# Score masks written by ScalarE into the scores' PSUM slot, in place of eight bfloat16 mask products a tile

## What is computed

```
mask = (it < jb) | (it > jb + w) | (jb == -1)
sim = jnp.einsum('bhwie,bhwje->bhwij', bq, bk2) * QK_SCALE
sim = jnp.where(mask, -jnp.finfo(sim.dtype).max, sim)
attn = jax.nn.softmax(sim, -1)
...
for i in range(DEPTH):
    x = attn_layer(shift_tokens(x), Wqkv[i], q_scale[i], k_scale[i], Wo[i]) + x
    x = ffn_layer(shift_tokens(x), ln_g[i], ln_b[i], W1[i], b1[i], W2[i], b2[i]) + x
```

## Time and profile before

| | |
|---|---|
| median of 3 runs | 3268.82 us (3267.74 to 3269.96) |
| the profiled execution's own time | 3261.97 us |
| its span | 3260.2 us |
| mean granted TensorE clock | 0.99 |
| busy share: TensorE, its weight loads, VectorE, ScalarE, GpSimd | 95%, 73%, 84%, 72%, 75% |
| instructions | 117935 |

### The profile page before, as it was taken

One profiled execution on the slowest core, in us unless ns is written; L12 is line 12 of the kernel. 1 busy time (PEld: TensorE's weight loads), 2 busy tenths in 40 slices (PEclk: granted clock), 3 DMA queues, 4 the chain that ended last, 5 costly groups with the idle time before them and its releaser, 6 DMA issues.

```text
span 3260.2 us, 117935 instructions
## 1 busy us (share of the span) xinstructions
PE 3101.1 (95%) x50166; PEld 2366.0 (73%) x50166; DVE 2741.3 (84%) x2887; ACT 2360.4 (72%) x3182; POOL 2442.6 (75%) x1239
## 2 busy tenths in 40 slices
PE   6999999999999999998888899999999999999998
PEld 5777787787777777775333677777777777777776
DVE  6888788888888888886999888788888888888886
ACT  5777777777777777666776677677777777777665
POOL 5778678687777777672899877777778778778764
PEclk8999999999999999999999999999999999999999
DMA  3333243243243243231000333333433433423322
GB/s 111 90 104 82 71 107 89 67 108 86 70 107 85 70 107 72 63 73 30 35 1 9 92 79 73 95 77 75 101 74 78 101 73 77 103 69 81 72 68 66
DMA packets 160006, 252.08 MB, mean 77 GB/s; under 512 B 50749, under 2 KB 52990, under 8 KB 157182
## 3 DMA queue, kind: packets, MB, share of 16 engines
q1 hardware_dynamic: 159486, 244.54, 30.0%
HBM read 35.67 MB, written 7.34 MB: 13 GB/s over the span
## 4 chain that ended last, share of the span: by engine, by line
PE 78%; POOL 6%; DVE 6%; issue 5%; ACT 4%; DMA 0%; SPq 0%; DVEq 0%; ACTq 0%; POOLq 0%
PE PS L327 14%; PE PS L428 10%; PE PS L230 10%; PE PS L232 9%; PE PS L231 9%; PE PS L379 8%; PE PS L543 3%; PE PS L502 2%; PE PS L503 2%; PE PS L504 2%; PE PS L389 2%; POOL ARENA L1908 2%; PE PS L487 2%; DVE ARENA L1715 2%; PE PS L459 1%
## 5 line engine op out<-in xcount | busy, mean ns | idle before, releaser
L1799 POOL TENSOR_TENSOR ARENA<-ARENA,RN 128x1024 f32<-128x1024 f32 x192 | 364.7, 1899 | 477.7 <-ACT RN L957 470.5
L230 PE MATMUL PS<-WL,XH 128*128 128x512 f32 x1536 | 673.5, 438 | 28.7 <-DVE ARENA L1404 24.1
L327 PE MATMUL PS<-C,ARENA 128*128 128x128 f32 x4608 | 621.0, 278 | 34.6 <-POOL ARENA L1799 11.2
L327 PEld LDWEIGHTS PS<-C,ARENA 128*128 128x128 f32 x4608 | 520.4, 142 | 161.5 <-issue 99.2
L232 PE MATMUL PS<-WH,XH 128*128 128x512 f32 x1536 | 608.9, 396 | 0.0
L231 PE MATMUL PS<-WH,XL 128*128 128x512 f32 x1536 | 604.4, 393 | 0.0
L1791 POOL TENSOR_TENSOR ARENA<-ARENA 128x1024 f32<-128x1024 f32 x192 | 469.2, 2444 | 167.8 <-DVE ARENA L1363 167.2
L1785 POOL TENSOR_TENSOR ARENA<-ARENA 128x1024 f32<-128x1024 f32 x192 | 460.0, 2396 | 13.0 <-DVE ARENA L1345 13.0
L1813 POOL TENSOR_TENSOR ARENA<-ARENA,RI 128x1024 f32<-128x1024 f32 x192 | 366.2, 1907 | 41.4 <-DVE RI L1415 31.3
L428 PE MATMUL PS<-ARENA 128*32 128x128 f32 x12288 | 378.6, 274 | 5.9 <-issue 1.7
L1807 POOL TENSOR_TENSOR ARENA<-ARENA,RN 128x1024 f32<-128x1024 f32 x192 | 372.6, 1940 | 10.4 <-ACT RN L957 10.4
(11 more groups left out here) (170 smaller groups left out, 6148.5 us busy)
## 6 DMA issues: line engine op xcount, KB each, us to landing
ARENA<-ARENA SPq DMA_DIRECT2D x1536, 64.0 KB
ARENA<-VT SPq DMA_DIRECT2D x1536, 64.0 KB
ARENA<-in_wqk SPq DMA_DIRECT2D x24, 512.0 KB, 5.9
ARENA<-in_wvo SPq DMA_DIRECT2D x6, 1024.0 KB, 6.1
MD<-ARENA SPq DMA_DIRECT2D x6, 1024.0 KB, 8.0
ARENA<-MD SPq DMA_DIRECT2D x6, 1024.0 KB, 9.7
ARENA<-in_w SPq DMA_DIRECT2D x12, 341.0 KB
ARENA<-in_w SPq DMA_DIRECT2D x12, 192.0 KB, 2.8
```

Source lines behind the costliest of these rows:

```text
L230: nc.tensor.matmul(o, XH[:, x], WL[:, s], start=True, stop=False)
L327: last = nc.tensor.transpose(PS[:, slot, 128 * j:128 * j + 128], src[:, 128 * j:128 * j + 128], ident)
L1799: nc.gpsimd.tensor_tensor(a, a, bc(RN[:, n % 2, 0:16], 64), ALU.mult).then_inc(q_nrm, 1)
```

## The change

`score_masks` and `MK` go, and with them VectorE's cast at the start. The host's constants now hold two masks in float32 of 128 rows by 64 columns, `mask` and `mask0` (the second for the first tile of the sequence). ScalarE copies one of them, broadcast over the 16 heads, into slot 3 (`set_masks`), and the score products add to what stands there. TensorE waits for that copy (`masks_set`) where it waited for what had freed the slot; those waits are ScalarE's now. `set_masks` stands at one of two places in a step of ScalarE: right behind k_evacuate (`early`), or, for tiles of class 3, tile 0 and the merge tiles, behind keep_merged. In the closing part the write of tile 95 (slot 0) stands ahead of the exponential of tile 94.

The additions rely on flags that TensorE keeps: a product with `start=True` marks its whole bank as not yet written. That is why the merge products and the closing transposes of slot 0 now set it only once a bank.

```diff
-        MK = sb("MK", [128, 128], BF16)
+        mask, mask0 = C[:, 1536:1600], C[:, 1600:1664]
...
                         last = nc.tensor.matmul(PS[:, 3, 512 * u + 128 * g:512 * u + 128 * g + 128], wv[a:b, w], wo[a:b, w],
-                                                start=True, stop=True, skip_group_check=True)
+                                                start=g == 0, stop=True, skip_group_check=True)
...
-            def score_masks(n, slot=3):
-                for win in range(4):
-                    pick = 32 * (n % NT == 0 and win == 0)
-                    for par in range(2):
-                        a, b = 64 * par, 64 * par + 64
-                        nc.tensor.matmul(
-                            PS[32 * win:32 * win + 32, slot, 512 * par:512 * par + 512], MK[a:b, pick:pick + 32],
-                            MK[a:b, 64:128].unsqueeze(1).broadcast_to([64, 8, 64]), start=True, stop=False,
-                            skip_group_check=True)
...
-                    if r == 0:
-                        pe.wait_ge(masks_set, 1)
-                if n:
-                    pe.wait_ge(vb_ev, n0 + n + 1)
-                if n % 4 == 3:
-                    after_chunk(pe, f_h[1], (n - 4) // 4)
-                if r == 0 and n < N - NT and n % NT in (5, 9):
-                    pe.wait_ge(mv_ev, 2 * (n // NT) + 3 + n % NT // 9)
-                score_masks(n)
+                pe.wait_ge(masks_set, n0 + n + 1)
                 score_tiles(n, range(8)).then_inc(S_done, 1)
...
-                transposes(0, KN[1], kT_done)
+                for j in range(8):
+                    last = nc.tensor.matmul(PS[:, 0, 128 * j:128 * j + 128], KN[1][:, 128 * j:128 * j + 128], ident,
+                                            start=j % 4 == 0, stop=True, is_transpose=True, skip_group_check=True)
+                last.then_inc(kT_done, 1)
...
+            def early(n):
+                return n and n % 4 != 3 and not (r == 0 and n < N - NT and n % NT in (5, 9))
...
+            def set_masks(n, slot=3):
+                if n == 0:
+                    act.wait_ge(i_done, 4 * r + 4)
+                elif n == 95:
+                    act.wait_ge(k_rot, n0 + 96)
+                    act.wait_ge(kT_ev, n0 + 96)
+                else:
+                    act.wait_ge(vb_ev, n0 + n + 1)
+                if n % 4 == 3 and 3 < n < 95:
+                    act.wait_ge(f_h[1], c0 + (n - 4) // 4 + 1)
+                if r == 0 and n < N - NT and n % NT in (5, 9):
+                    act.wait_ge(mv_ev, 2 * (n // NT) + 3 + n % NT // 9)
+                m = mask0 if n % NT == 0 else mask
+                act.activation(heads(PS[:, slot, :]), m.unsqueeze(1).broadcast_to([128, H, 64]), ACT.Copy).then_inc(masks_set, 1)
...
                 k_evacuate(s - 19)
+                set_masks_early(s - 19)
                 gelu0(s - 23)
                 gelu1(s - 23)
                 gelu2(s - 23)
                 q_square(s - 17)
                 keep_merged(s - 19)
+                set_masks_late(s - 19)
                 ffn_square(s - 22)
...
             k_evacuate(95, 0)
+            set_masks(95, 0)
             exponentials(94)
...
-                nc.vector.tensor_copy(MK[:, :], C[:, 1536:1664]).then_inc(masks_set, 1)
```

More of the change, by code:

```diff
@@ L581, in finish_tiles @@
                 tile(car_ev, 95)
-                score_masks(95, 0)
+                tile(masks_set, 95)
                 score_tiles(95, range(8), 0).then_inc(S_done, 1)
@@ L1017, in exponentials, with set_masks_early, set_masks_late @@
                                scale=8.0).then_inc(exp_done, 1)
+            def early(n):
+                return n and n % 4 != 3 and not (r == 0 and n < N - NT and n % NT in (5, 9))
+            def set_masks_early(n):
+                if 0 <= n < N and early(n):
+                    set_masks(n)
+            def set_masks_late(n):
+                if 0 <= n < N and not early(n):
+                    set_masks(n)
+            def set_masks(n, slot=3):
[12 more added lines that the diff above has]
+                act.activation(heads(PS[:, slot, :]), m.unsqueeze(1).broadcast_to([128, H, 64]), ACT.Copy).then_inc(masks_set, 1)
             def p_evacuate(n, slot=2):
@@ L2080, in shape_constants @@
     ok = (i <= j) & (j <= i + 32)
[L2081 to L2084, removed]
+    mask = np.tile(np.where(ok, 0, -1e30), (4, 1))
+    mask0 = mask.copy()
+    mask0[:32, :32] = -1e30
+    masks = [mask, mask0]
     eye, mean = np.eye(128), np.full((128, 128), 1 / 128)
```

## The result

| | median, us | range, us | runs |
|---|---|---|---|
| before | 3268.28 | 3262.83 to 3269.96 | 4 |
| after | 3370.06 | 3354.23 to 3377.44 | 4 |

The ratio is 1.0305, with a 95% interval of 1.0286 to 1.0325: slower by 3.1%. I forecast 3287 us with a range up to 3306. The direction was right and the size was not: 102 us between the medians where I had 18.6. The profiled execution after took 3369.95 us, 108.0 more than the 3261.97 of the one before.

What follows compares the result with a forecast made beforehand. TensorE, its matmuls busy for 95% of the span, was taken as the bound. 28.5 - 18.9 + 0 + 4.9 + 4.1 = +18.6 us on 3261.97, with 6.85 for the median, gave 3287 us; range 3267 to 3306.

Steps and rivals of the forecast that it cites:

- 0.22 to 0.23 us off TensorE a tile: Removing the eight mask products lets TensorE's first score product start 0.22 to 0.23 us sooner in each tile.
- The write takes 1.03 us and pushes by 0.92: ScalarE's mask copy into PSUM takes 1.03 us and delays ScalarE work behind it by up to 0.92 us.
- Class 3 loses 0.62 us: Tiles with n modulo 4 = 3: scores wait for the write behind the square of q; 46 x 0.62 = 28.5 us lost.
- Merge tiles lose 0.41: Ten first-stack tiles, n mod 16 = 5 or 9: the write behind keep_merged delays scores 0.41 us, 4.1 us in all.
- Class 0: zero, and 4.9 us in the tiles with n mod 16 = 4: Tiles with n modulo 4 = 0: later rotation cancels the gain in 36; ten behind a weight split lose 0.49 us each.
- Classes 1 and 2 have slack, so no wait: Early tiles, n modulo 4 = 1 or 2: slack of 1.9 and 2.7 us covers the push; 86 x 0.22 = 18.9 us gained.
- The sum: All tile gains and losses over the whole run together: +18.6 us, giving 3287 us, 0.6% slower.
- (1): Term of the sum: TensorE's time from the last product ahead of masks or scores to the first score product.
- (2): Term of the sum: TensorE's k_project waiting for the rotation on VectorE.
- score products far from 1.46 us: Sign that would show the forecast wrong: a tile's 64 score products on TensorE no longer taking about 1.46 us.
- The clock rival: New 0.9 us TensorE waits in ten weight-split tiles lower the granted clock: 24 us more, 3311 us; chance 0.04.

Runs made afterwards that it cites:

- e1: Kernel before without its eight mask products a tile and nothing in their place, so no mask is applied; 3238.77 us, ratio 0.9905.
- e5: Kernel after plus 153 tiny filler products in 47 tiles, shifting where score products start in the instruction blocks; 3296.25 us, ratio 1.0094 to before.
- e6: Kernel before plus 414 tiny filler products in 20 tiles, shifting where score products start in the instruction blocks; 3275.43 us, ratio 1.0027.
- e2: Kernel before plus one wait ahead of the mask products, on ScalarE's square of q for tile n + 2; 3350.59 us, ratio 1.0246.

## Why the prediction was wrong in its size

Point by point, after against before, from the two traces unless said otherwise.

- *0.22 to 0.23 us off TensorE a tile.* Right: 0.229 in e1; in the 86 tiles of classes 1 and 2, -0.233 each (I had -0.22).
- *The write takes 1.03 us and pushes by 0.92.* Right: median 1.033 us of 192, starts 0.92 to 0.95 apart. An estimate from the figures of the Trainium skill (ScalarE: Activation LUTs, "What ACT_TABLE_LOAD costs"), 186 ns and 0.833 ns a column, was 1.04; the trace agrees.
- *Class 3 loses 0.62 us.* Right: +0.61 us a tile in the 46 tiles of the sum, and the wait of 0.77 by L1028 stands where I said (I had about 0.9).
- *Merge tiles lose 0.41.* Somewhat low: +0.60 in each of ten.
- *Class 0: zero, and 4.9 us in the tiles with n mod 16 = 4.* Right in kind: k_project waits for the rotation 7.4 us in 26 class 0 tiles (I had some 13: the 36 x 0.22 that I let cancel and the 4.9), against 9.4 gained.
- *Classes 1 and 2 have slack, so no wait.* Not quite: 16 class 1 tiles wait 5.2 us together.
- *The sum.* 16.8 us for (1) and (2) together, and 20.8 between e5 and e6, against 18.6.

The step that failed is the one that said nothing: after "the first score product starts then" I took the 64 products behind it at their old duration. I had written that nothing says they get any quicker, and in the list of signs that score products far from 1.46 us would prove me wrong, but I gave the case no price above zero. I had taken the new wait as one on execution alone, and left out that the instructions behind it arrive later too. Yet the profile before had it. The row `PE PS L379 <- issue` of 24.4 us in 29 tiles was the largest of TensorE's waits within a tile of attention, beside the 24.1 of the earlier trace rows that I did read; I passed over it since it names no partner. Had I asked what ends an "issue" wait, the uneven duration of the same 64 products and the q8 transfers were there to see. That term, at nothing in my sum, measured +46 us, and the clock that fell with it some 40 more.

The clock rival had the right end (slower by much, 3311 us, 4%), the wrong cause and place. I let it start from semaphore waits of 0.9 us in ten tiles. Those waits alone did nothing that can be told from the noise: in e5, which has 41.3 us of them, the clock lost 36.1 us against 32.6 before. In the class 3 tile shown above it fell at the end of a stall of 2.40 us that followed the wait of 0.77; over the run it cost another 41 us by (4), 32 of them at stalls.

What the change did, then: TensorE's wait for the masks is met 1.3 us later in the mean than those that stood there before (0.73 us ahead of the first score product instead of 2.04), even where TensorE does not stand idle for it. Up to there the queue cannot read on. The hold is shown by e2, which adds only the wait, and by the transfers, which start 1.1 us later in the stalled tiles; that a transfer is asked for when the reading passes some point of a block is argued from them. What stays open is that point itself, since tiles with the same start in a block stall in one place and not in another, and 5 us or more of the 108.

## What to carry to other kernels

A wait can cost where no engine is seen waiting. It also holds back the instructions behind it, and in front of a burst of tiny products (here 256 instructions in 1.5 us) it should be met early. Read "issue" rows like any other wait and ask which position of the stream they sit at. A stall that recurs in some repetitions of the same code and never in others can come from the stream's blocks. A new wait in front of such a burst is worth a run of its own, with the wait alone and no other edit (as e2).

## What the runs showed of the chip that I had not expected

- Score products stall only where a block of 256 instructions ends (position 192 or 193 in this count). They go on 2.2 to 3.2 us after the transfer of the next block starts (225 stalled tiles of six kernels, median 2.6).
- A semaphore wait that no row shows as a wait cost 80 us over 192 tiles (e2).
- A tiny product (64 rows, 1 column) takes 65 ns in a row of 25 and 0.15 us alone. Wait instructions that are already met stand 106 ns apart in a row; some 100 in a row (200 calls, two to an instruction) leave TensorE idle for 7 to 11 us.
- Where a stall of 2.40 us stood in dense work the granted clock of the 20 us around it was 0.93, and with one of 6.79 us 0.83. Stalls removed, the clock is back (0.989 in e5, 0.978 after).
- A float32 write of ScalarE into PSUM of 1024 columns takes 1.03 us, the same as the way out, and products with `start=False` add to it.
